# Delta-rule stages of a vision tower: one table switch fewer per stage, projections behind the values, more inverse rows ahead of the weighing

## What is computed

```python
def step(S, inp):
    qt, kt, vt, at, gkt = inp
    Sp = S * jnp.exp(gkt)[..., None]
    u = jnp.einsum('bhk,bhkv->bhv', at, Sp) + vt
    S = Sp + jnp.einsum('bhk,bhv->bhkv', kt, u)
    o = jnp.einsum('bhk,bhkv->bhv', qt, S)
    return (S, o)
q, k, v = silu(x @ Wq), silu(x @ Wk), silu(x @ Wv)
log_f = jax.nn.log_sigmoid(x @ Wf)
gamma = -jax.nn.sigmoid(x @ Wgamma)
k = l2norm(k.reshape(b, n, H, HD))
a = k * gamma[..., None] * jnp.exp(gk)      # gk is log_f, repeated
```

## Time and profile before

| | |
|---|---|
| median of 3 runs | 1997.47 us (1995.56 to 2000.2) |
| profiled execution | 1989.77 us, of which the span of the core's work is 1988.0 us |
| busy in the span | PE 1708.2 us, DVE 1108.5, ACT 656.6, POOL 314.5 |
| stages of the delta rule | from 1303.0 us to about 1819 us of the span |
| five full stages | 1392.26 to 1687.34 us |

### The profile page before, as it was taken

One profiled execution on the slowest core, in us unless ns is written; L12 is line 12 of the kernel. 1 busy time (PEld: TensorE's weight loads), 2 busy tenths in 40 slices (PEclk: granted clock), 3 DMA queues, 4 the chain that ended last, 5 costly groups with the idle time before them and its releaser, 6 DMA issues. The chain is left out here.

```text
span 1988.0 us, 51796 instructions
## 1 busy us (share of the span) xinstructions
PE 1708.2 (86%) x22689; PEld 1517.3 (76%) x22689; DVE 1108.5 (56%) x2379; ACT 656.6 (33%) x1347; POOL 314.5 (16%) x284
## 2 busy tenths in 40 slices
PE   4677786799999999999999999876888888757589
PEld 4466675579988999989999999745877777756468
DVE  3655555674545555455555465566445555543885
ACT  3334534433322233232223232163333333223142
POOL 0232232520000000000000000052322223200530
PEclk9888988899999999999999999877666656655579
DMA  4100000100100000000101000100000000001001
GB/s 135 60 2 1 0 0 1 67 22 1 43 1 22 22 22 22 22 22 1 44 1 43 1 1 1 36 1 2 4 4 4 3 4 4 4 4 48 1 11 41
DMA packets 10070, 36.01 MB, mean 18 GB/s; under 512 B 3056, under 2 KB 6152, under 8 KB 7304
## 3 DMA queue, kind: packets, MB, share of 16 engines
q1 hardware_dynamic: 9864, 32.96, 4.8%
HBM read 30.47 MB, written 2.49 MB: 17 GB/s over the span
## 5 line engine op out<-in xcount | busy, mean ns | idle before, releaser
L1042 ACT ACTIVATE hidden<-bank,moe_b 128x512 f32<-128x512 f32 (+1 forms) x320 | 213.3, 668 | 537.1 <-PE bank L934 524.5
L951 PE MATMUL bank<-moe_w2h,hidden_hi 128*128 128x256 f32 x1216 | 345.7, 284 | 0.0
L951 PE MATMUL bank<-moe_w2l,hidden_hi 128*128 128x256 f32 x1216 | 344.0, 283 | 0.0
L951 PE MATMUL bank<-moe_w2h,hidden_lo 128*128 128x256 f32 x1216 | 343.9, 283 | 0.0
L934 PE MATMUL bank<-x_hi,moe_w1h 128*128 128x512 f32 (+1 forms) x640 | 243.8, 381 | 2.9 <-ACT hidden L1042 2.8
L934 PE MATMUL bank<-x_lo,moe_w1h 128*128 128x512 f32 (+1 forms) x640 | 242.5, 379 | 0.0
L934 PE MATMUL bank<-x_hi,moe_w1l 128*128 128x512 f32 (+1 forms) x640 | 242.0, 378 | 0.0
L951 PEld LDWEIGHTS bank<-moe_w2h,hidden_hi 128*128 128x128 f32 x1216 | 233.1, 192 | 6.0 <-DVE residual L1076 4.3
L1076 DVE SCALAR_TENSOR_TENSOR residual<-bank,gates,residual 128x256 f32<-128x256 f32 x152 | 73.4, 484 | 290.4 <-PE bank L951 290.4
L951 PEld LDWEIGHTS bank<-moe_w2l,hidden_hi 128*128 128x128 f32 x1216 | 233.2, 192 | 1.2
L951 PEld LDWEIGHTS bank<-moe_w2h,hidden_lo 128*128 128x128 f32 x1216 | 233.2, 192 | 0.0
(11 more groups left out here) (287 smaller groups left out, 3357.3 us busy)
## 6 DMA issues: line engine op xcount, KB each, us to landing
moe_w<-in_moe_w SPq DMA_DIRECT2D x16, 1024.0 KB, 4.8
patches<-in_patches SPq DMA_DIRECT2D x8, 864.0 KB, 4.6
out<-residual SPq DMA_DIRECT2D x19, 128.0 KB, 1.7
ffn_w<-in_ffn_w SPq DMA_DIRECT2D x2, 1024.0 KB, 6.4
att_w<-in_att_w SPq DMA_DIRECT2D x1, 1536.0 KB, 5.9
delta_w<-in_delta_w SPq DMA_DIRECT2D x1, 1280.0 KB
tok_w<-in_tok_w SPq DMA_DIRECT2D x1, 768.0 KB, 4.1
delta_wvf<-in_delta_wvf SPq DMA_DIRECT2D x1, 272.0 KB
```

Of the source, the lines that this page charges most:

```text
L951: mm = nc.tensor.matmul(bank[4 + n % 3][:, 0:D], left, right, start=(i == 0), stop=(i == len(passes) - 1))
L1042: nc.scalar.activation(H[:, i % 4, 0:n], bank[i % 4][:, 0:n], ACT.Relu, bias=b1[:, x, f:f + 1]).then_inc(acted, 1)
```

## The change

The calls are the same, and so is the arithmetic. What changes is their order on PE, ACT and DVE; POOL's list is left alone. ACT starts a stage with the sigmoid table, does all sigmoids, switches once to exp and ln, and only then runs `forget_logs`. Line numbers after the change are four lower from L1795 on, DVE's by four, POOL's by six.

```diff
@@ PE
             low_part(1)
-            first_half(0)
             project(0)
-            first_half(1)
             project(1)
             low_part(2)
-            remainder(0)
+            first_half(0)
             project(2)
             low_part(3)
-            remainder(1)
             project(3)
             low_part(4)
+            first_half(1)
+            remainder(0)
+            key_norm(0)
+            remainder(1)
+            key_norm(1)
             second_half(0)
             decay(0)
             second_half(1)
             decay(1)
-            key_norm(0)
-            key_norm(1)
             output()
             decay(2)
+            inverse_out(0)
             score(0)
             decay(3)
-            inverse_out(0)
+            inverse_out(1)
+            score(1)
             decay(4)
-            score(1)
             decay(5)
-            inverse_out(1)
+            score(2)
             decay(6)
-            score(2)
             decay(7)
             inverse_out(2)
             score(3)
@@ ACT
-            nc.scalar.preload_act_table_set("natural_log_exp_and_others")
+            nc.scalar.preload_act_table_set("sigmoid_and_others")
             for p in range(IP):
                 forget_parts(p)
-            forget_logs()
-            nc.scalar.preload_act_table_set("sigmoid_and_others")
-            sigmoid_values(0)
-            sigmoid_values(1)
+                sigmoid_values(p)
+            sigmoid(0)
+            sigmoid(1)
             first_back(0)
-            sigmoid(0)
-            sigmoid_values(2)
-            first_back(1)
-            sigmoid(1)
-            sigmoid_values(3)
-            padded(0)
             sigmoid(2)
-            padded(1)
             sigmoid(3)
             for i in range(len(spans)):
                 low_high(i)
+            first_back(1)
             nc.scalar.preload_act_table_set("natural_log_exp_and_others")
+            forget_logs()
+            padded(0)
+            padded(1)
+            inverse_norms()
             solution(0)
             decay(0)
             solution(1)
             decay(1)
-            inverse_norms()
             high_out(0)
             high_out(1)
@@ DVE
             for t in range(1, 5):
                 inverse_row(t)
-            log_forget()
-            inverse_row(5)
+            for p in range(IP):
+                values_of(p)
             silu_of(0)
-            values_of(0)
-            values_of(1)
             silu_of(1)
-            values_of(2)
-            values_of(3)
-            with_values(0)
             silu_of(2)
-            with_values(1)
             silu_of(3)
             gate_parts()
             step_scale()
-            for t in range(6, 10):
-                inverse_row(t)
+            inverse_row(5)
+            with_values(0)
+            log_forget()
+            inverse_row(6)
             bounded(0)
+            with_values(1)
             bounded(1)
-            for t in range(10, 13):
+            for t in range(7, 14):
                 inverse_row(t)
             low_out(0)
             low_out(1)
-            inverse_row(13)
             inverse_row(14)
             weigh(0)
             weigh(1)
             inverse_row(15)
+            weigh(2)
+            weigh(3)
             unit_key(0)
             unit_key(1)
             inverse_row(16)
-            weigh(2)
-            weigh(3)
             inverse_row(17)
+            weigh(4)
+            weigh(5)
             inverse_row(18)
-            for b in range(4, CB):
-                weigh(b)
+            weigh(6)
+            weigh(7)
```

More of the change, by code:

```diff
@@ L1803, in _ @@
             decay(2)
+            inverse_back(0)
             decay(3)
-            inverse_back(0)
+            inverse_back(1)
             decay(4)
             decay(5)
-            inverse_back(1)
             decay(6)
```

## The result

The kernel after takes 2081.69 us (median of 4 runs, 2079.07 to 2084.95), the kernel before 1996.51 us beside it (1993.22 to 2000.2): 1.0427 times as long [1.0403, 1.0451], or 85.2 us more. The forecast was 2073, in a range of 2040 to 2108. In the profiled execution the span grew from 1988.0 to 2077.3 us, by 89.3.

A forecast was written before the change was run, and what follows sets the result against it. In a full stage PE hardly stops until the output ends, then DVE is the chain. Five full stages 57.5, stages 1, 2, 8, 9 and 0 +6, +8, +4, -1, +1: 75.5 on 1997.5 gives 2073 us, range 2040 to 2108.

The forecast's parts named there:

- The key norms: Full stage, PE: late log_forget delays POOL's squares, so second_half(0) starts 9.7 us later; output starts 7.5 later (6.4 to 8.6).
- X: End of remainder(0) in the full stage read: 19.2 us before, taken as 21.7 after, bounds 20.6 and 22.8.
- the "issue" wait: PE's wait among packed small matmuls may grow: +0.7 us a full stage, from nothing to another 1.56.
- The tail: Behind the output, DVE waits before weigh(2) (+3.5) and weigh(6) (+1.0), less row 13: +3.3 us, range +1.5 to +4.5.
- the −1.2 for row 13: Behind the output on DVE: row 13 goes ahead into idle time, saving 1.2 us.
- The sum: Full stage 8.2 + 3.3 = 11.5 us longer, five of them 57.5; with the other stages 75.5.
- Stage 1: Key norm at 17.5 us of the stage (+5), ACT's inverse_norms +1: +6, range 4 to 7.
- The table switch: ACT: eleven loads fewer, 14.1 us, hidden by PE's queue with 4.8 slack before project(2); removal gives nothing.
- The clock falls as well: Rival: new PE gaps lower the granted clock, 5.4 us a stage, 27 more in all, 2100 us; chance 0.2.
- Part of the wait is absorbed: Rival: issue waits vanish, remainder(0) ends early, tail +1.5; 7 us a full stage, sum 49, 2046 us; chance 0.13.
- It is faster: Rival: load leaves the path, inverse rows fill DVE's idle time; 14.1 us less, 1983 us; chance 0.03.
- no change: Rival: gain and loss meet, total time within 0.2% of before; chance 0.02.

The follow-up runs named there:

- Experiment 1: Changed kernel with POOL running both squares, then the clears, ahead of its steps: 2036.65 us, 1.022 times the kernel before.
- experiment 6: Changed kernel with POOL's squares ahead of its steps and the old order behind the output, row 13 kept early: 1996.57 us, 1.0009 times the kernel before.
- experiment 3: Changed kernel with the key norms put back behind the second halves and decays, bounded and inverse_norms with them: 2036.34 us, 1.0202 times the kernel before.
- Experiment 4: Changed kernel with the old order behind the output on PE, ACT and DVE, row 13 kept ahead of it: 2038.63 us, 1.0223 times the kernel before.
- Experiment 5: Kernel before with only the change's order behind the output, row 13 ahead of it: 2028.65 us, 1.0173 times the kernel before.
- experiment 10: Changed kernel with POOL's squares ahead of its steps and the tail of experiment 8: 1984.45 us, 0.9957 times the kernel before.
- experiment 8: Kernel before with row 13 early, score(3) ahead of inverse_out(2), and later weighings behind rows 17 and 18: 1984.44 us, 0.9949 times the kernel before.
- experiment 9: Kernel before with only the change's table switches, so logs behind all sigmoids and log_forget later on DVE: 2005.16 us, 1.0066 times the kernel before.
- Experiment 12: Kernel before with two more real table loads per stage, behind the sigmoid load: 1999.76 us, 1.0033 times the kernel before.
- experiment 11: Version of experiment 8 with both unit_key calls moved from behind row 15 to behind row 18: 1976.09 us, 0.9918 times the kernel before.

## Why the prediction was right

**The key norms: the mechanism and nearly the size.** The step said that `key_norm(0)` starts at X + 6.5 and `second_half(0)` at X + 13.0 = 34.7. In the stage read above X is 21.62 (21.7 was taken), the key norm starts 6.13 later, and `second_half(0)` is at 34.76. Over the five full stages it moved from 25.0 to 34.6 on average, and the output's start by 7.2 (7.5). The missing 0.4 of the first wait is POOL's: clear and square took 1.61, not 1.95. Experiment 1 undoes this part alone and gives 45 us.

**The output: the "issue" wait nearly right, a term missing.** The term was +0.7 in a range of nothing to 1.56. The stops in the output took 1.8 before and 2.6 after on average, +0.8. But the output as a whole took 4.75 before and 6.06 after, +1.3. The other 0.5 is in its matmuls, for which the sum had nothing. The clock granted in the output was 1.00, 0.98, 0.78, 0.50 and 0.81 in the five stages before, and is 0.50, 0.50, 0.79, 0.50 and 0.50 after. It is 0.50 in all five of experiments 1 and 6, where PE waits for no square, and 0.74 to 0.83 in experiment 3, which has the four key norms right ahead of the output again. So it goes with what stands ahead of the output, and not with the gaps.

**The tail: mis-sized, +5.3 for +3.3.** That is beyond its own range of +1.5 to +4.5. From the end of the output to the start of the last four weighing instructions the full stages took 17.9 before and 23.2 after, on average. In the two stages read above, `weigh(2)` has +3.6 (3.5) and `weigh(6)` 2.45 for 1.55, +0.9 (1.0), as predicted.

The step that failed is the −1.2 for row 13. The same paragraph says that `weigh(0)` starts as before, and it nearly does: 3.91 behind the end of the output, 3.83 before. Then moving row 13 away from in front of it can shorten nothing. DVE spends the 1.2 in a wait for the score (0.73) and in row 14 (1.09 for 0.57). Experiment 4, which has the old tail with row 13 ahead, is no shorter for it. The rest was only in the range, as a disturbance by POOL on more rows: the keys 2.27 for 0.85 and row 16 0.68 for 1.70, together +0.4. One stage of the five has 25.5: there an "issue" stop of 1.6 falls into the decay ahead of `inverse_out(0)`, and `weigh(0)` waits 3.73. Experiment 5 has the same waits without the front half, and costs 35 us; experiment 4 saves 43.

**The sum.** 7.2 + 1.3 + 5.3 = 13.8 for a full stage, measured 13.8, predicted 11.5; over five stages that is 11 of the 14 us by which the span grew more than 75.5. Stages 1, 2, 8 and 9 were put at +6, +8, +4 and −1 and came out at +7.7, +10.4, +4.1 and −2.2.

**Stage 1: near by luck.** The log does come behind the sigmoids and the load, as said. But the first key norm was put at 17.5 of the stage and starts at 15.6: it waits for the first square alone, and the sum had both squares ahead of it. So this part is +3.2 and not +5. From there to the end of the stage 4.5 more are added, where +1 was predicted for ACT: the key norms take 1.2 longer at the lower clock, and experiment 4, with the old tail, has 1.3 less of it. The rest was not separated. Two errors of opposite sign make +7.7 look like +6.

**The table switch: hidden where it was said to be, not everywhere.** The kernel after has one load less a stage; in experiment 10 the whole front half, the saved loads with it, is worth nothing measurable against experiment 8, and in experiment 9 saving them alone costs 11 us. Experiment 12 confirms the slack of the full stages, with 2.57 put into the 4.8. For stages 1 and 2 "its removal gives nothing" does not hold: there the loads are on the path. The sum for stage 1 had the load's 1.3 in it, and what the moved log costs is more: in experiment 9 the first decay waits 4.57 in each of the two, and stage 1 is 4.4 longer (stage 2 is not).

Each load follows the one before at 1.29, and the sigmoid follows the last at 1.29. The Trainium skill ("ScalarE: Activation LUTs", What ACT_TABLE_LOAD costs) has some 1380 ns of drain behind a load; in three loads in a row there is room for none.

**The rivals.** *The clock falls as well:* not in the full stages. They had 0.67, 0.67, 0.65, 0.62 and 0.65 before and have 0.64, 0.62, 0.67, 0.62 and 0.64 now, and PE's busy time in them fell from 249.0 to 240.5. In the stage read above, the matmuls of values and projections start 0.24 apart at first and 0.13 to 0.14 apart from 1494.04 on, and the granted clock goes from 0.50 to 1.00 there: the dense run gets the higher clock before the gaps come. Behind them it is 0.50 up to the output, as it was before. In the output it fell, but in experiment 1, which has no gaps, as well (see above); that is at most 0.5 a stage. In stages 1 and 2 the rival is right in kind: the key norms, at 1.00 before, run at 0.50 behind the wait and take 1.2 longer each time. *Part of the wait is absorbed:* no, the tail and the issue waits were above the middle, not below. (By its own terms this rival's full stage is +6.3, not 7, and its sum 46 instead of 49.) *It is faster* and *no change* needed a square that is done in time; experiment 1 shows that even then the tail keeps it slow, and experiment 6 that with both repaired it is "no change".

## What to carry to other kernels

In a kernel of hand-written lists, moving a call forward on one engine moves its producer's place in the producer's list into play: before moving it, walk that list and count what stands ahead of the producer and what that waits for. A consumer that is put right behind its producer, here `weigh` behind `score`, turns hidden latency into a wait; leave independent work between them. And a saved load or switch is worth what the chain of waits says it is, which may be less than what has to be moved to save it. A row that is taken out from in front of a call gives nothing if the call starts at the same time as before.

## What the hardware showed that was not expected

**VectorE held by GpSimd.** A DVE instruction that reads two operands from SBUF took up to 1.0 us longer for each POOL step (1.21) that ran at the same time: two keys 0.85 alone, 1.87 with one hold, 2.27 with more; row 16 0.69 alone, 1.69 or 1.70 held; row 15 0.62 alone and 1.0 where less of the step was left. In experiment 8 the step ends at 1556.85 and the held row 0.54 later. The weighings, which read one operand from PSUM, took 1.61 or 1.62 for four in every place, beside a step or not. The Trainium skill ("SBUF — State Buffer", SBUF: two separate sides, and Who interferes with whom) says that a VectorE instruction with two SBUF inputs contends with a GpSimd instruction that reads SBUF, and that the later one waits for the whole of the earlier. These rows agree. What the holds cost the kernel is less than their length: experiment 11 takes 6 us of them out of the five full stages, and its tails are 1.6 us shorter, since a new wait for ACT's decay takes 3.3 us back.

**The supply of instructions.** Packed small matmuls stop at places that are some 128 recorded ones apart: 1.76 us of them, then 1.98; 1.61, then 2.13; 1.51, then 1.12. The places are fixed in the program. In the output of the five full stages the kernel before stops behind 172, 243, 186, 129 and 200 matmuls; the kernel after stops there too, and in four of the five also 128 matmuls earlier. Large matmuls right ahead of the output let it pass that earlier place (the kernel before and experiment 3). Where the stop falls decides what it costs: the stage whose stop fell into a decay was 3 us longer in its tail. The Trainium skill ("Runtime: NRT & Kernel Launch", Instruction fetch mechanics) says that an engine's program is refilled in blocks of 16 KiB, or 256 instructions, and that this is mostly hidden. 128 matmuls with their 128 weight loads are such a block, so the spacing agrees; "mostly hidden" does not hold for these runs. That the stops are the refill is argued from this and from the label "issue", and was not tested by itself.
